# A transformer block on one core: head and tail of the instruction streams in another order, and some attention outputs in other PSUM banks

## The chip, the cores and the metric

The kernel runs on one core of a Trainium2 chip. The core has five engines, each of which works through its own list of instructions in order: TensorE (PE, matrix products), VectorE (DVE), ScalarE (ACT), GpSimd (POOL) and SyncE (SP), which issues the DMA transfers here. They meet through semaphores: an instruction counts one up when it is done, and another engine waits for a count. The metric is the device time of one execution in microseconds; the median of three runs counts.

## The reference

A pre-layernorm block on x of 1024 tokens by 256 features, all in float32:

```python
x = x + attention(layernorm(x))   # 16 heads of 128, rotary q and k, window of 128 keys, softmax, output projection wo
x = x + ffn(layernorm(x))         # 256 -> 1024, exact gelu, 1024 -> 256; weights rounded to -1, 0, 1
```

A query sees only the 128 keys up to its own position, so a tile of 128 queries needs the keys of its own tile and of the one before.

## The kernel before

Each float32 product is made of three products of halves: an operand is split into a `hi` part (a cast, on ScalarE) and a `lo` part (the rest, a subtraction on VectorE or GpSimd). So a tensor that TensorE is to use costs two more instructions on two engines: `qkhi`/`qklo` for the weights of q and k of a head, `vhi`/`vlo` for the value weights of a pair of heads, `xt_hi`/`xt_lo` for the transposed input, `rothi`/`rotlo` for rotated q or k, `ot_hi`/`ot_lo` for the attention output. All engines have their order written out by hand.

The work runs over 64 chunks and 64 steps. A chunk m projects q or k of a head for half of the tokens (`project(m)`, L385). VectorE multiplies it by sine (`times_sin`, L717, L719) and cosine (`times_cos`), SP swaps the halves of the sine product by two DMA transfers (`swap`, L287), the sum is `rotate` (on VectorE, L735, for the first two chunks, on GpSimd, L949, for the rest), then come `rothi` on ScalarE (L589) and `rotlo` (VectorE L740 for the first two, GpSimd L954 after). A step n handles 256 queries of one head: `scores(n)` on TensorE (L435), `merge(n)` on VectorE (L748, L751, L754: the windowed scores and their maximum), `exps(n)` on ScalarE (L594), `inverse_sum(n)` on VectorE (L759), `scale_probs(n)` on ScalarE (L601), `transpose_probs(n)` on TensorE (L446), `mask_pt(n)` on VectorE (L765), `weigh_v(n)` on TensorE (L460), then `ot_hi(n)` on ScalarE (L613) and `ot_lo(n)` on VectorE (L772). In step n TensorE does the scores of n, the transposition and weighing of n - 1, the projection of chunk n + 4 and a filler, if there is one: `project_v` (L400, the values of 256 tokens for a pair of heads; ScalarE's `copy_v` takes them out of the bank) or `project_out` (L417, the output projection; VectorE's `add_out`, L778, adds it to x). Steps 2 to 6 have no filler; from step 7 on nearly every step has one. `LP` is 56, the first step of the last pair of heads; `PAIRS` is 8.

PSUM has eight banks: PR0, PR1 (projections), SC0, SC1 (scores), PT (transposed probabilities), OT (attention outputs), and VO0, VO1 (values and output projections, by turns). `weigh_v(n)` waits until `ot_lo(n - 1)` has read OT.

After the last step come the second layernorm (`tile_stats` L690, `moments` L696, L698, `rsqrt` on GpSimd L931, `normalise` L703), the transposition of x (`transpose_x`, L358), the two layers of the feed-forward part (`ffn1` L488, `ffn2` L507) and its splitting (`ghi` L802, `glo` L807), twice, once for each half of the tokens. The first of these stand among the last steps already.

The head of GpSimd's list, the part before its loop over the steps, reads

```python
rsqrt(0, 0); pool.wait_ge(xn_ready, 4); qklo(0); rsqrt(0, 1); vlo(0)
pool.wait_ge(rot_done, 2); rotate(2); qklo(1); pool.wait_ge(rotlo_done, 2)
```

and ScalarE's: `qkhi(0)`, `xt_hi(0, 0)`, `vhi(0)`, `copy_v(0)`, `xt_hi(0, 1)`, `copy_v(1)`, `rothi(0)`, `qkhi(1)`, `rothi(1)`, `rothi(2)`.

Of the kernel before, what the change touches and what calls it, by code (L numbers as in the profile page):

```python
# [5 lines left out]
P = 128  # L6
# [10 lines left out]
def preln_block_kernel(nc, x, wq, wk, wv, wo, w1t, b1, w2t, b2, cos_t, sin_t, in_prev, mask_t, ident, out):  # L17
    T, D = x.shape
    HD = P
# [15 lines left out]
    with ExitStack() as ctx:  # L35
# [186 lines left out]
        def before_in_bank(kind, i):  # L222
            at = in_banks.index((kind, i))
            earlier = [f for f in in_banks[:at] if f[1] % 2 == i % 2]
            return earlier[-1] if earlier else None

        def half_of(c):

            return slice((c // 2) * HALF, (c // 2 + 1) * HALF)
# [18 lines left out]
        def _(sp):  # L248
# [49 lines left out]
            load_table(0, cos_sb)  # L298
            load_table(1, sin_sb)
            load_table(1, cos_sb)  # L300
            load_head(1)
            swap(0)
            sp.dma_start(in_prev_sb[:], in_prev).then_inc(mask_in, 16)
            sp.dma_start(mask_sb[:].rearrange("p b q -> p (b q)"), mask_t).then_inc(mask_in, 16)
            swap(1)
            swap(2)
            sp.wait_ge(qklo_done, 1)
            load_head(2)
            swap(3)
            sp.wait_ge(vlo_done, 1)  # L310
# [32 lines left out]
        def _(pe):  # L343
# [46 lines left out]
            def project_v(v):  # L390
                p, c = v // 4, v % 4
                if c == 0:
                    pe.wait_ge(vlo_done, p + 1)
                bank_free("v", v)
                for i in range(2):
                    t = 2 * c + i
                    n = 0
                    for kd in range(KD):
                        for xt, wt in ((xT_hi, v_lo), (xT_lo, v_hi), (xT_hi, v_hi)):
                            last = mm(VO[v % 2][:, i * 256:(i + 1) * 256], xt[:, kd, t * P:(t + 1) * P], wt[:, kd],  # L400
                                      start=(n == 0), stop=(n == 3 * KD - 1))
                            n += 1
                last.then_inc(v_done, 1)
# [45 lines left out]
            def weigh_v(n):  # L449
                head, j = step(n)  # L450
                a = head % 2
                pe.wait_ge(pt_masked, n + 1)
                pe.wait_ge(v_copied, 4 * (head // 2) + j + 1)
                if n > 0:
                    pe.wait_ge(otlo_done, n)
                for i in range(2):
                    t = 2 * j + i
                    b0 = 1 if t == 0 else 0
                    for b in range(b0, 2):
                        last = mm(OT[:, i * P:(i + 1) * P], v_sb[:, t - 1 + b, a * HD:(a + 1) * HD],  # L460
                                  probsT[:, i, b], start=(b == b0), stop=(b == 1))
                last.then_inc(pv_done, 1)
# [59 lines left out]
            project(2, KD)  # L522
            project(3)
            for n in range(STEPS):
                scores(n)
                if n == MEANS_AT:
                    means_of_abs()
                if n > 0:
                    transpose_probs(n - 1)
                if n + 4 < CHUNKS:  # L530
                    project(n + 4)
                fill(n)
                if n == STEPS - 1:
                    transpose_x(1, 0)
                if n > 0:
                    weigh_v(n - 1)
            ffn1(0)
# [20 lines left out]
        def _(act):  # L558
# [51 lines left out]
            def ot_hi(n):  # L610
                head, j = step(n)
                act.wait_ge(pv_done, n + 1)
                copy(oT_hi(head)[:, 2 * j * P:(2 * j + 2) * P], OT[:, 0:256]).then_inc(othi_done, 1)  # L613

# [18 lines left out]
            xt_hi(0, 0)  # L633
            vhi(0)
            copy_v(0)
            xt_hi(0, 1)
            copy_v(1)
            rothi(0)
            qkhi(1)
            rothi(1)  # L640
            rothi(2)
            for n in range(STEPS):
                p, s = n // 8, n % 8
                if n >= 2:
                    ot_hi(n - 2)
                exps(n)
                if n == STEPS - 1:
                    xt_hi(1, 0)
                    ot_hi(n - 1)
                    nc.scalar.preload_act_table(ACT.Gelu)  # L650
                if n > 0:
                    for kind, i in fills(n - 1):
                        if kind == "v":
                            copy_v(i)
                scale_probs(n)
                if n + 3 < CHUNKS:
                    rothi(n + 3)
# [24 lines left out]
        def _(dve):  # L682
# [85 lines left out]
            def ot_lo(n):  # L768
                head, j = step(n)
                dve.wait_ge(othi_done, n + 1)  # L770
                ts = slice(2 * j * P, (2 * j + 2) * P)
                tt(oT_lo(head)[:, ts], OT[:, 0:256], oT_hi(head)[:, ts].bitcast(F32), ALU.subtract).then_inc(otlo_done, 1)  # L772

# [56 lines left out]
            times_cos(0)  # L830
            normalise(0, 1)
            times_sin(1)
            times_cos(1)
            rotate(0)
            xt_lo(0, 1)
            rotlo(0)
            rotate(1)
            dve.wait_ge(sin_in[1], 32)
            times_sin(2)
            rotlo(1)  # L840
            dve.wait_ge(cos_in[1], 16)
            times_cos(2)
            dve.wait_ge(nothing_set, 1)
            dve.wait_ge(mask_in, 32)
            nc.vector.copy_predicated(no_prev[:], in_prev_sb[:], nothing[:]).then_inc(no_prev_set, 1)
            times_sin(3)
            times_cos(3)
            dve.wait_ge(no_prev_set, 1)
            for n in range(STEPS):
                if n == STEPS - 2:  # L850
                    add_out(4 * PAIRS - 3)
                    tile_stats(1, 2)
                    tile_stats(1, 3)
                if n == STEPS - 1:
                    ot_lo(n - 2)
                    normalise(1, 0)
                merge(n)
# [4 lines left out]
                if 1 < n < STEPS - 1:  # L862
                    ot_lo(n - 2)
                if n == STEPS - 2:
                    moments(1, 0)
                if n + 4 < CHUNKS:
                    times_sin(n + 4)
                if n >= LP + 4:
                    for kind, w in fills(n - 1):
                        if kind == "o" and w != 4 * PAIRS - 3 and w != 4 * PAIRS - 4:  # L870
                            add_out(w)
                inverse_sum(n)
                if n + 4 < CHUNKS:
                    times_cos(n + 4)
                if 0 < n < LP + 4:
                    for kind, w in fills(n - 1):
                        if kind == "o":
                            add_out(w)
                if n == STEPS - 3:
                    add_out(4 * PAIRS - 4)  # L880
                    tile_stats(1, 0)
                    tile_stats(1, 1)
                if n == MEANS_AT:
                    thresholds()
# [10 lines left out]
            glo(1)  # L895
            add_out(4 * PAIRS - 2)
            tile_stats(1, 4)
            tile_stats(1, 5)
            ghi(2)
            glo(2)  # L900
            add_out(4 * PAIRS - 1)
            tile_stats(1, 6)
            tile_stats(1, 7)
            moments(1, 1)
            glo(3)
            ghi(4)
# [18 lines left out]
        def _(pool):  # L925
# [41 lines left out]
            pool.wait_ge(xn_ready, 4)  # L967
            qklo(0)
            rsqrt(0, 1)
            vlo(0)  # L970
            pool.wait_ge(rot_done, 2)
            rotate(2)
            qklo(1)
            pool.wait_ge(rotlo_done, 2)
# [60 lines left out]
```

## Time and profile before

| | |
|---|---|
| median of three runs | 361.02 us (360.62 to 361.49) |
| the profiled execution | 360.54 us |
| its span, first to last instruction | 358.8 us |
| TensorE busy | 340.5 us, 95% |
| VectorE, ScalarE, GpSimd busy | 263.8, 208.1, 223.5 us (74%, 58%, 62%) |
| mean granted clock of TensorE | 0.990 |

Busy shares are means over the span; products on TensorE are pipelined, so a busy TensorE is not one at its peak. Times within the profile count from the first instruction of the span.

### The profile page before, as it was taken

The page shows a single profiled execution, that of the slowest core. Times are in us where ns is not written, and L with a number is a line of the kernel's source. Part 1 is how long each engine was busy: PE and PEld are TensorE (multiplying, and loading weights), DVE is VectorE, ACT ScalarE, POOL GpSimd, SP SyncE. Part 2 cuts the span into 40 slices and gives each one's busy share as a digit, 9 for nine tenths or more (in the row PEclk, how much of TensorE's full clock was granted, in tenths as well). Part 3 has the DMA queues.
Part 4 walks back from the last instruction along what each step waited for, and adds up shares of the span by engine and source line. Part 5 has one row for each costly group of instructions (what it writes and reads, how often), then busy time and mean ns, then how long its engine had stood idle before and what let it go on. Part 6 is the DMA issues. An engine that isn't in the chain of part 4 may idle for free.

```text
span 358.8 us, 6923 instructions
## 1 busy us (share of the span) xinstructions
PE 340.5 (95%) x2410; PEld 315.1 (88%) x2410; DVE 263.8 (74%) x607; ACT 208.1 (58%) x626; POOL 223.5 (62%) x182
## 2 busy tenths in 40 slices
PE   7849999999999999999999999999999999898996
PEld 6738778999999999999999999999999999877986
DVE  4874777668766886788788986787678766788681
ACT  2243676677777556655665566556665666365180
POOL 2326778667767678799879987585867656231300
PEclk9997999999999999999999999999999999999999
DMA  7734466543333333333333333333322231000001
GB/s 220 188 95 114 117 164 197 130 102 78 92 83 86 80 84 84 88 81 89 88 90 88 90 88 90 90 89 90 88 61 58 61 88 31 0 3 0 31 29 58
DMA packets 29025, 31.25 MB, mean 87 GB/s; under 512 B 3392, under 2 KB 20288, under 8 KB 28992
## 3 DMA queue, kind: packets, MB, share of 16 engines
q1 hardware_dynamic: 28992, 30.82, 33.7%
q8 instruction: 19, 0.31, 0.4%
q14 instruction: 14, 0.11, 0.1%
HBM read 12.98 MB, written 1.05 MB: 39 GB/s over the span
## 4 chain that ended last, share of the span: by engine, by line
PE 84%; DVE 9%; POOL 2%; issue 2%; DMA 1%; ACT 1%; DVEq 0%; SPq 0%; POOLq 0%
PE PR L385 22%; PE OT L460 15%; PE VO L400 13%; PE SC L435 12%; PE VO L417 11%; PE PT L446 3%; PE PR L488 2%; PE SC L488 2%; PE VO L507 1%; DVE probsT L765 1%; PE SC L507 1%; DVE stats L690 1%; DVE SC L751 1%; DVE gT_lo L807 1%; DVE gT_lo L772 1%
## 5 line engine op out<-in xcount | busy, mean ns | idle before, releaser
L954 POOL TENSOR_TENSOR gT_lo<-turn,gT_hi 128x512 fp32r<-128x512 f32 x62 | 81.7, 1318 | 42.9 <-ACT gT_hi L589 42.7
L949 POOL TENSOR_TENSOR turn<-turn,swapped 128x512 f32<-128x512 f32 x62 | 80.2, 1293 | 38.2 <-DMA swapped<-by_sin 37.9
L594 ACT ACTIVATE probs<-SC,negmax 128x128 f32<-128x128 f32 x128 | 45.8, 363 | 61.9 <-DVE negmax L754 61.9
L460 PE MATMUL OT<-probsT,v_sb 128*128 128x128 f32 x480 | 64.6, 276 | 3.1 <-DVE gT_lo L772 2.7
L601 ACT ACTIVATE probs<-probs,rinv 128x128 f32<-128x128 f32 x128 | 44.5, 395 | 38.2 <-DVE rinv L759 38.2
L460 PEld LDWEIGHTS OT<-probsT,v_sb 128*128 128x128 f32 x480 | 58.9, 191 | 6.0 <-DVE probsT L765 6.0
L385 PE MATMUL PR<-xT_hi,qk_lo 128*128 128x512 f32 x128 | 56.2, 439 | 5.1 <-POOL qk_lo L936 3.7
L751 DVE COPY_PREDICATED SC<-in_prev_sb,SC 128x256 f32<-128x256 int32 x48 | 20.6, 428 | 45.7 <-PE SC L435 45.5
L385 PE MATMUL PR<-xT_hi,qk_hi 128*128 128x512 f32 x128 | 51.0, 398 | 0.0
L385 PE MATMUL PR<-xT_lo,qk_hi 128*128 128x512 f32 x128 | 50.4, 394 | 0.0
L765 DVE TENSOR_TENSOR probsT<-PT,mask_sb 128x512 f32<-128x512 f32 x64 | 43.6, 681 | 1.2 <-PE PT L446 1.2
L589 ACT CAST gT_hi<-turn 128x512 fp32r<-128x512 f32 x64 | 38.9, 607 | 8.5 <-POOL turn L949 7.6
L435 PE MATMUL SC<-gT_hi,gT_lo 128*128 128x256 f32 (+1 forms) x128 | 41.1, 321 | 0.4 <-DVE gT_lo L740 0.4
L400 PE MATMUL VO<-v_lo,xT_hi 128*128 128x256 f32 x128 | 36.7, 287 | 1.0 <-POOL v_lo L940 1.0
L417 PE MATMUL VO<-o_lo,gT_hi 128*128 128x256 f32 x128 | 36.3, 284 | 1.0 <-DVE xres L778 1.0
L400 PE MATMUL VO<-v_hi,xT_hi 128*128 128x256 f32 x128 | 36.6, 286 | 0.0
L400 PE MATMUL VO<-v_hi,xT_lo 128*128 128x256 f32 x128 | 36.5, 285 | 0.0
L417 PE MATMUL VO<-o_hi,gT_hi 128*128 128x256 f32 x128 | 36.0, 282 | 0.0
L435 PE MATMUL SC<-gT_lo,gT_hi 128*128 128x256 f32 (+1 forms) x128 | 36.0, 281 | 0.0
L435 PE MATMUL SC<-gT_hi 128*128 128x256 f32 (+1 forms) x128 | 35.9, 281 | 0.0
L417 PE MATMUL VO<-o_hi,gT_lo 128*128 128x256 f32 x128 | 35.9, 281 | 0.0
L385 PEld LDWEIGHTS PR<-xT_hi,qk_lo 128*128 128x128 f32 x128 | 24.3, 190 | 8.5 <-POOL qk_lo L936 3.9
(114 smaller groups left out, 839.1 us busy)
## 6 DMA issues: line engine op xcount, KB each, us to landing
swapped<-by_sin SPq DMA_DIRECT2D x128, 128.0 KB, 2.3
qk_raw<-in_wq SPq DMA_DIRECT2D x16, 128.0 KB, 2.6
qk_raw<-in_wk SPq DMA_DIRECT2D x16, 128.0 KB, 2.4
v_raw<-in_wv SPq DMA_DIRECT2D x8, 256.0 KB, 3.1
o_raw<-in_wo SPq DMA_DIRECT2D x8, 256.0 KB, 2.9
xres<-in_x SPq DMA_DIRECT2D x4, 256.0 KB, 3.2
w_raw<-in_w1t SPq DMA_DIRECT2D x4, 256.0 KB, 3.0
w_raw<-in_w2t SPq DMA_DIRECT2D x4, 256.0 KB, 3.0
```

Of the source, the lines that this page charges most:

```text
L385: last = mm(PR[m % 2][:], wt[:, c % 2, kd], xt[:, kd, half_of(c)], start=(n == 0), stop=(n == 3 * KD - 1))
L400: last = mm(VO[v % 2][:, i * 256:(i + 1) * 256], xt[:, kd, t * P:(t + 1) * P], wt[:, kd], start=(n == 0), stop=(n == 3 * KD - 1))
L417: last = mm(VO[w % 2][:, i * 256:(i + 1) * 256], ot[:, t * P:(t + 1) * P], wt[:, a], start=(n == 0), stop=(n == 5))
L435: last = mm(SC[n % 2][:, o0:(i + 1) * 256], q[:, t * P:(t + 1) * P], k[:, k0 * P:(t + 1) * P], start=(p_ == 0), stop=(p_ == 2))
L460: last = mm(OT[:, i * P:(i + 1) * P], v_sb[:, t - 1 + b, a * HD:(a + 1) * HD], probsT[:, i, b], start=(b == b0), stop=(b == 1))
L589: copy(rot_hi(head, c % 2)[:, half_of(c)], turn[m % 4][:]).then_inc(rothi_done, 1)
L594: nc.scalar.activation(probs[n % 2][:, i], SC[n % 2][:, i * 256 + P:(i + 1) * 256], ACT.Exp, bias=negmax[:, n % 2, i:i + 1], accum_out=row ...
L601: last = nc.scalar.activation(probs[n % 2][:, i], probs[n % 2][:, i], ACT.Copy, scale=rinv[:, n % 2, i:i + 1])
L751: nc.vector.copy_predicated(sc[:, :, 1], in_prev_sb[:].unsqueeze(1).broadcast_to([P, 2, P]), sc[:, :, 0]).then_inc(merged, 1)
L765: tt(probsT[:], PT[:, 0:256].rearrange("p (i q) -> p i q", i=2).unsqueeze(2).broadcast_to([P, 2, 2, P]), mask_sb[:].unsqueeze(1).broadcast ...
L949: tt(turn[m % 4][:], turn[m % 4][:], swapped[m % 2][:], ALU.add).then_inc(rot_done, 1)
L954: tt(rot_lo(head, c % 2)[:, half_of(c)], turn[m % 4][:], rot_hi(head, c % 2)[:, half_of(c)].bitcast(F32), ALU.subtract).then_inc(rotlo_don ...
```

## The change

No instruction is added or removed, and no size changes. On SP the load of head 1 goes ahead of the second cosine table, the two masks ahead of the first swap, and the load of head 2 ahead of the third swap. On TensorE `project(3)` and the filler of step 0 go behind `scores(0)`, and in step 63 the transposition of x goes ahead of the filler. `weigh_v` of steps 2 to 5 writes the banks VO0 and VO1 instead of OT, and `ot_hi` and `ot_lo` read them there; its waits and those of `project_v(4)` and `project_v(5)` follow. On ScalarE, VectorE and GpSimd the instructions ahead of the loop and those of the last steps stand in another order.

```diff
+        def ot_bank(n):
+            return VO[n % 2] if 2 <= n <= 5 else OT
...
             load_table(1, sin_sb)
+            load_head(1)
             load_table(1, cos_sb)
-            load_head(1)
-            swap(0)
             sp.dma_start(in_prev_sb[:], in_prev).then_inc(mask_in, 16)
             sp.dma_start(mask_sb[:].rearrange("p b q -> p (b q)"), mask_t).then_inc(mask_in, 16)
+            swap(0)
             swap(1)
-            swap(2)
             sp.wait_ge(qklo_done, 1)
             load_head(2)
+            swap(2)
...
# project_v(v), TensorE
+                if v in (4, 5):
+                    pe.wait_ge(otlo_done, v + 1)
                 bank_free("v", v)
...
# weigh_v(n), TensorE
-                if n > 0:
-                    pe.wait_ge(otlo_done, n)
+                if n in (2, 3):
+                    bank_free("v", n + 2)
+                elif n > 0:
+                    pe.wait_ge(otlo_done, {4: 3, 5: 4, 6: 2}.get(n, n))
-                        last = mm(OT[:, i * P:(i + 1) * P], v_sb[:, t - 1 + b, a * HD:(a + 1) * HD],
+                        last = mm(ot_bank(n)[:, i * P:(i + 1) * P], v_sb[:, t - 1 + b, a * HD:(a + 1) * HD],
...
# TensorE
             project(2, KD)
-            project(3)
             for n in range(STEPS):
                 scores(n)
+                if n == 0:
+                    project(3)
+                    fill(0)
                 if n == MEANS_AT:
                     means_of_abs()
                 if n > 0:
                     transpose_probs(n - 1)
                 if n + 4 < CHUNKS:
                     project(n + 4)
-                fill(n)
                 if n == STEPS - 1:
                     transpose_x(1, 0)
                 if n > 0:
+                    fill(n)
                     weigh_v(n - 1)
...
# ScalarE (ot_hi reads ot_bank(n))
             vhi(0)
+            qkhi(1)
             copy_v(0)
             xt_hi(0, 1)
+            rothi(0)
+            rothi(1)
             copy_v(1)
-            rothi(0)
-            qkhi(1)
-            rothi(1)
-            rothi(2)
             for n in range(STEPS):
                 p, s = n // 8, n % 8
                 if n >= 2:
                     ot_hi(n - 2)
+                if n == STEPS - 1:
+                    xt_hi(1, 0)
                 exps(n)
                 if n == STEPS - 1:
-                    xt_hi(1, 0)
                     ot_hi(n - 1)
...
                 scale_probs(n)
+                if n == 0:
+                    rothi(2)
...
# VectorE (ot_lo reads ot_bank(n))
             times_cos(0)
-            normalise(0, 1)
             times_sin(1)
             times_cos(1)
+            normalise(0, 1)
             rotate(0)
+            rotate(1)
             xt_lo(0, 1)
             rotlo(0)
-            rotate(1)
-            dve.wait_ge(sin_in[1], 32)
-            times_sin(2)
             rotlo(1)
-            dve.wait_ge(cos_in[1], 16)
-            times_cos(2)
             dve.wait_ge(nothing_set, 1)
             dve.wait_ge(mask_in, 32)
             nc.vector.copy_predicated(no_prev[:], in_prev_sb[:], nothing[:]).then_inc(no_prev_set, 1)
-            times_sin(3)
-            times_cos(3)
+            dve.wait_ge(sin_in[1], 32)
+            times_sin(2)
+            dve.wait_ge(cos_in[1], 16)
+            times_cos(2)
             dve.wait_ge(no_prev_set, 1)
             for n in range(STEPS):
                 if n == STEPS - 2:
                     add_out(4 * PAIRS - 3)
                     tile_stats(1, 2)
                     tile_stats(1, 3)
+                    moments(1, 0)
                 if n == STEPS - 1:
                     ot_lo(n - 2)
-                    normalise(1, 0)
                 merge(n)
...
                 if 1 < n < STEPS - 1:
                     ot_lo(n - 2)
+                if n == 0:
+                    times_sin(3)
+                    times_cos(3)
                 if n == STEPS - 2:
-                    moments(1, 0)
+                    normalise(1, 0)
                 if n + 4 < CHUNKS:
                     times_sin(n + 4)
-                if n >= LP + 4:
-                    for kind, w in fills(n - 1):
-                        if kind == "o" and w != 4 * PAIRS - 3 and w != 4 * PAIRS - 4:
-                            add_out(w)
                 inverse_sum(n)
...
-                if 0 < n < LP + 4:
+                if n <= LP + 4:
                     for kind, w in fills(n - 1):
-                        if kind == "o":
+                        if kind == "o" and n > 0:
                             add_out(w)
+                if n == LP + 4:
+                    add_out(4 * PAIRS - 7)
                 if n == STEPS - 3:
                     add_out(4 * PAIRS - 4)
                     tile_stats(1, 0)
                     tile_stats(1, 1)
+                if n == STEPS - 2:
+                    add_out(4 * PAIRS - 6)
...
             add_out(4 * PAIRS - 2)
+            ghi(2)
+            glo(2)
+            glo(3)
             tile_stats(1, 4)
             tile_stats(1, 5)
-            ghi(2)
-            glo(2)
             add_out(4 * PAIRS - 1)
             tile_stats(1, 6)
             tile_stats(1, 7)
             moments(1, 1)
-            glo(3)
...
# GpSimd
             qklo(0)
+            vlo(0)
             rsqrt(0, 1)
-            vlo(0)
             pool.wait_ge(rot_done, 2)
+            qklo(1)
             rotate(2)
-            qklo(1)
             pool.wait_ge(rotlo_done, 2)
```

## Rows read from the trace of the kernel before

**Rows 1.** The page: TensorE's granted clock, 40 slices of 9 us, in tenths.
```profile
PEclk9997999999999999999999999999999999999999
```

**Rows 2.** Busy time by stretches: engine columns, then clock, DMA share, GB/s.
```profile
24.00:28.00 4.00, 0.60 (x2) 0.50 (x3) 1.51 (x5) 1.33 (x5) 3.13 (x3) 0.64 0.77 215
48.00:60.00 12.00, 11.22 (x77) 9.80 (x77) 9.64 (x22) 8.26 (x27) 10.71 (x9) 1.00 0.60 168
80.00:120.00 40.00, 40.00 (x294) 37.70 (x293) 30.15 (x73) 27.96 (x92) 27.34 (x23) 1.00 0.35 87
```

**Rows 3.** Waits of TensorE: total us, times, longest.
```profile
PE PR L385 <- POOL qk_lo L936: 3.7, 1, 3.7
PE OT L460 <- DVE gT_lo L772: 2.7, 7, 0.5
PE PR L385 <- DVE xT_lo L711: 1.4, 1, 1.4
...
PE VO L417 <- DVE xres L778: 1.0, 1, 1.0
PE VO L400 <- POOL v_lo L940: 1.0, 1, 1.0
```

**Rows 4.** The chain that ended last, head: start, length, what.
```profile
13.97 3.13 PE VO L400 x24
17.10 0.78 PE SC L358 x7
...
19.36 1.64 PE PR L385 x6
...
24.87 1.26 POOL turn L949
26.13 1.23 POOL qk_lo L936
...
27.40 2.93 PE PR L385 x6
30.33 2.20 PE VO L400 x12
...
33.47 1.39 PE PR L385 x6
34.86 1.43 PE VO L400 x12
...
36.96 0.73 PE SC L435 x6
```

**Rows 5.** Timeline of VectorE: start, length, what.
```profile
22.00 0.69 DVE L740 TENSOR_TENSOR gT_lo<-turn,gT_hi 128x512 fp32r<-128x512 f32 x1
```

**Rows 6.** Timeline of ScalarE.
```profile
31.17 0.69 ACT L601 ACTIVATE probs<-probs,rinv 128x128 f32<-128x128 f32 x2 [3.68 <-DVE rinv L759]
31.77 0.60 ACT L589 CAST gT_hi<-turn 128x512 fp32r<-128x512 f32 x1
```

**Rows 7.** The chain that ended last, one of steps 2 to 6.
```profile
38.51 0.68 DVE probsT L765
39.19 0.34 DVE gT_lo L772
...
39.67 1.13 PE OT L460 x8
```

**Rows 8.** The chain that ended last, tail.
```profile
305.25 0.61 DVE xres L778
...
311.27 1.14 PE OT L460 x8
...
313.27 1.29 DVE xnorm L703 x4
...
315.39 0.81 ACT probs L594 x4
...
316.71 0.70 DVE xT_lo L711
```

More of the change, by code:

```diff
@@ L612, in ot_hi @@
                 act.wait_ge(pv_done, n + 1)
-                copy(oT_hi(head)[:, 2 * j * P:(2 * j + 2) * P], OT[:, 0:256]).then_inc(othi_done, 1)
+                copy(oT_hi(head)[:, 2 * j * P:(2 * j + 2) * P], ot_bank(n)[:, 0:256]).then_inc(othi_done, 1)
             def abs_sums(i):
@@ L771, in ot_lo @@
                 ts = slice(2 * j * P, (2 * j + 2) * P)
-                tt(oT_lo(head)[:, ts], OT[:, 0:256], oT_hi(head)[:, ts].bitcast(F32), ALU.subtract).then_inc(otlo_done, 1)
+                tt(oT_lo(head)[:, ts], ot_bank(n)[:, 0:256], oT_hi(head)[:, ts].bitcast(F32), ALU.subtract).then_inc(otlo_done, 1)
             def add_out(w):
```

## The prediction

> **What bounds the kernel now.** I read the page first, then the busy time by stretches, the waits of TensorE, and the chain of work that ended last. From 80 to 120 us TensorE is busy 40.00 of 40.00 us [rows 2], and the stretches up to 280 us look the same: the middle can only move as a whole. TensorE's own work is not touched by the change, so all there is to win is idle TensorE time and low clock at the head (before about 60 us) and at the tail (after 300 us).
>
> At the head there are three losses. First, TensorE waits 3.7 us, once, for `qk_lo` of head 1 [rows 3]. The chain says why: the GpSimd product `rotate(2)` starts at 24.87, released by the DMA swap of chunk 2, and only behind it, at 26.13, runs the subtraction that makes `qk_lo`; `project(4)` starts at 27.40 [rows 4]. Second, the clock: its mean is 0.64 in 24 to 28 us [rows 2], and the page's row of clocks has its one dip, a 7, in the fourth slice, 27 to 36 us [rows 1], right behind that idle time. 0.5 is the level 1.2 GHz, 1.0 is 2.4 GHz. Third, 2.7 us in seven waits for `gT_lo`, VectorE's `ot_lo` [rows 3]: the weighing of the values has one bank, OT, and cannot write it until `ot_lo` of the step before has read it.
>
> **The head, worked out.** Times are the span's, before to after.
>
> *Projection of the values.* `vlo(0)` goes ahead of `rsqrt(0,1)` on GpSimd, so the 1.0 us wait for `v_lo` [rows 3] goes: 13.97 becomes 13.0 [rows 4]. The price is that the second half's rstd comes about one GpSimd operation (1.25 us [rows 4]) later; it is hidden, because VectorE now works through the rotation products of chunk 1 before `normalise(0, 1)`, and TensorE needs the result only after 3.13 us of value products. If that cover were too short, the loss is at most the 1.0 us just won. So `project(2)` starts at 19.36 - 1.0 = 18.4 and ends at 20.0 [rows 4].
>
> *scores(0).* It no longer stands behind `project(3)`, but it needs `rotlo(1)`. VectorE has one more half of `xT_lo` and two `rotlo` after the release of `project(2)` at 18.25: three operations of 0.69 us [rows 5], partly overlapped, give 20.2. Then `scores(0)` with the extra 0.25 us of a product after a wait (1.64 against 1.39 [rows 4]) ends at 21.15; with `project(3)` 1.39, values 1.43, `project(4)` 1.39 [rows 4] the next, `scores(1)`, starts at 25.4. `project(4)` does not wait, since `qklo(1)` now waits only for the second rotation, which stands ahead of `xt_lo(0, 1)` on VectorE and so is done before 18, and for its cast, which is moved up on ScalarE as its load is on the SP queue. Before, `scores(1)` came after 30.33 + 2.20 = 32.53. The lead is 7.1 us. Clock included: the two groups at 1.2 GHz cost 2.93 - 1.64 = 1.3 and 2.20 - 1.43 = 0.8, that is 2.1 us of the 7.1.
>
> *What is late next.* `rothi(2)` is moved behind `scale_probs(0)` on ScalarE. That one waits for the reciprocal, which stands on VectorE behind `times_sin(4)`, which needs `project(4)` (done at 25.4). So: `times_sin(4)` to 26.1, scaling (0.69 [rows 6], with some 0.15 of handing over) to 26.95, `rothi(2)` 0.60 [rows 6] to 27.5, and then in order on GpSimd and ScalarE `rotlo(2)`, `rotate(3)`, `rothi(3)`, `rotlo(3)`: three GpSimd operations of 1.25 and one cast of 0.60, with hand-overs 4.6 us, to 32.1. `scores(2)` needs `rotlo(3)`. TensorE has work meanwhile until about 30.8 (a wait of 1 us for the scaled probabilities, then 0.22 for two transpositions, an estimate from 0.78 for seven [rows 4], 1.39, 1.43 and a weighing of less than 1.13). So it waits about 1.3 us and starts `scores(2)` at 32.1 instead of 36.96, with 0.25 for starting after a wait: lead 4.6 us. Behind `rothi(3)` on ScalarE the exponentials of step 1 queue, and `weigh_v(1)` keeps its wait on OT; I count no more than the lead of `scores(2)` there.
>
> *Steps 3 to 6.* `weigh_v(2)` to `weigh_v(5)` write VO0 and VO1, and need only `mask_pt`. In a step the mask product begins at 38.51 and lasts 0.68, then `ot_lo` 0.34, then the weighing starts at 39.67 [rows 7]. Without `ot_lo` in front, the weighing may start 0.34 earlier; the wait of one step is 2.7/7 = 0.39, so 0.05 is left. Four steps: 1.36 us. Bounds: 0 if the rotation (GpSimd, two operations each step and a third in every second one, 2.5 to 3.75 us against a new step of 3.5) becomes the limit, 4 x 0.39 = 1.56 above. I take 1.36, since over two steps GpSimd needs 6.25 of 7. The new waits cost nothing: the banks are idle here (the next values come at step 7), the copy of values 2 and 3 is a step or two old, and `ot_lo(2)` to `ot_lo(5)` are each done a step before the bank's next user. Lead after step 7: 4.6 + 1.36 = 6.0 us.
>
> *SP's queue.* Head 1 ahead of the second cosine table, and both masks ahead of the first swap, let transfers go sooner that nobody waited for; the swaps wait for VectorE's products anyway. `load_head(2)` ahead of `swap(2)` is issued while SP waits for `times_sin(2)`. Nothing, bounded by one transfer's issue.
>
> **A rule against it.** The row: after 3.7 us without work the clock fell, while after the 1.4 us wait for `xT_lo` ahead of `project(2)` it was still full (the slices up to 27 us show a 9) [rows 1, 3]. The Trainium skill, "TensorE: Matmul & The Clock Gate", section "What's actually happening", says that throttled is the default and activity releases it. By that rule read strictly, the new head, which has three waits of about 1 us where it had one long one, could fall to 1.2 GHz as well; by the row it does not, and the sum stands. That is a rival below, priced from rows.
>
> **The tail.** Four moves, one chain. (a) `add_out(25)` goes a step earlier. Now it runs from 305.25 to 305.86 [rows 8] and TensorE waits 1.0 for it [rows 3]; afterwards the same product waits for `ot_lo(59)`, which ends at 305.25, so 0.6 is won. (b) `moments(1, 0)` goes ahead of `merge(62)`, which takes some of this back, about 0.1: `weigh_v(61)` comes at 310.75 instead of 311.27 [rows 8]. (c) `normalise(1, 0)` leaves its place ahead of `merge(63)` and follows `ot_lo(60)`: 310.6 + 1.29 [rows 8] = 311.9. The reciprocal of step 62 now queues behind it, so scaling ends at 312.8 and TensorE, which would be free at 312.5, waits 0.4 for it. (d) The transposition of x comes before the last filler: about 1.0 us (0.78 for seven [rows 4], and the release), to 314.0; two casts of 0.60 on ScalarE [rows 6] to 315.1; only then the exponentials of step 63, 0.81 [rows 8]. VectorE's reciprocal of step 63 stands ahead of `xt_lo(1, 0)`, so that starts at 316.0, against 316.71 [rows 8]. Lead 0.7. Bounds: 0, if the reciprocal or the table load falls later, and 1.29, if the whole `normalise` leaves the chain. Behind it `glo(3)` comes earlier, but VectorE has the same operations between the last `add_out` and the last `glo`, and TensorE needs that: the lead carries on, nothing is added.
>
> **Sum.** 6.0 + 0.7 = 6.7 us. The profiled execution took 360.54 us, of which its span is 358.8; 360.54 - 6.7 = 353.8. The median of the runs lies 0.48 above the profiled execution, so I forecast 354.3 us.
>
> **Rivals.**
> 1. *As worked out*: 354.3, own range 353.0 to 355.8. Chance 0.58.
> 2. *The clock falls again, or the rotation stays the limit to step 7*: the first costs up to 2.1 us, the second takes the 1.36 us. For it: three waits close together and GpSimd nearly full. Against: the waits are short. 355.8 to 357.8. Chance 0.20.
> 3. *Nothing is given back at `scores(2)`*, because `rotate(3)` or the scaling comes sooner than I have it: 7.1 instead of 4.6, that is 351.8. For it: all hand-overs above are rounded up. Against: `rothi(2)` is where it is. Chance 0.12.
> 4. *Slower: the low clock holds through the steps without fillers.* At 1.2 GHz a projection costs 1.3 us more; scores (0.73) and a weighing (about 0.9) would at most double, so a step costs up to 2.9 us more. Steps 1 to 6 would give 354.3 + 17 = 371. It decides from 6.7/2.9 = 2.3 such steps on. Against: in 48 to 60 us TensorE is idle a little in each step, 11.22 busy of 12, at a full clock [rows 2]. Chance 0.05. The rule named above would work in this way.
> 5. *The change does not do what it says*: `project(4)` waits all the same, because `qkhi(1)` or `rotate(1)` is late. Then the head wins the 1.0 and little else; within 1 us of 361. Chance 0.05.
>
> The range that leaves out no more than two in ten is 351.9 to 357.6. A measurement of this kernel can tell about 0.2% from no change, 0.7 us; faster by more than that: 0.90, within it: 0.04, slower: 0.06.
>
> **What the new profile would show.** Right: no wait of TensorE for `qk_lo`; granted clock 1.0 between 24 and 36 us; `scores(1)` at about 25, a wait of 1 to 2 us for `gT_lo` of the rotation at about 31; waits of the weighing for `gT_lo` down from seven to three or so, for `probsT` instead of it some 0.05; the first half of `xt_lo(1, 0)` 6.7 us earlier than 316.71. Wrong if: the clock row dips again; GpSimd runs without gaps from 32 to 54 us and TensorE waits for it at each second step; or the waits after 300 us are as long as now. The weakest term is the wait at `scores(2)`.

## The result and the profile after

The changed kernel takes 354.96 us (median of four runs, 354.6 to 356.06) against 360.82 us of the kernel before beside it: ratio 0.9844, 95% interval 0.9813 to 0.9875, 5.9 us. Forecast were 354.3 us and a range of 351.9 to 357.6. The profiled span went from 358.8 to 352.9 us. One run of all that are reported here, of the kernel with three banks, took 476.35 us at a mean granted clock of 0.659, and no comparison below uses it.

The page of the changed kernel: its span, busy time by engine, and the row of granted clocks in tenths, which answers to [rows 1].

```profile
span 352.9 us, 6925 instructions
...
PE 340.2 (96%) x2410; PEld 314.6 (89%) x2410; DVE 263.5 (75%) x607; ACT 208.1 (59%) x626; POOL 224.0 (63%) x182
...
PEclk9999999999999999999999999999999999999999
```

TensorE runs the same 2410 instructions, and the 7 in the fourth slice is gone. The busy time by stretches answers to [rows 2].

```profile
24.00:28.00 4.00, 3.13 (x19) 2.54 (x18) 2.52 (x6) 1.20 (x3) 1.63 (x2) 1.00 0.78 211
...
48.00:60.00 12.00, 11.56 (x81) 10.34 (x80) 8.98 (x22) 8.79 (x28) 10.25 (x9) 1.00 0.64 172
...
80.00:120.00 40.00, 40.00 (x296) 37.74 (x295) 30.16 (x73) 27.74 (x90) 26.91 (x22) 1.00 0.33 82
```

From 24 to 28 us TensorE worked 0.60 us before and works 3.13 now, at a full clock. The middle is full in both, so what is won at the head stays won. The waits of TensorE answer to [rows 3].

```profile
PE OT L468 <- DVE gT_lo L784: 1.6, 3, 0.6
PE PT L452 <- ACT probs L611: 1.5, 3, 0.9
PE VO L515 <- DVE gT_lo L819: 1.5, 2, 0.9
PE PR L389 <- DVE xT_lo L723: 1.4, 1, 1.4
PE SC L441 <- POOL gT_lo L967: 1.3, 1, 1.3
```

The wait for `qk_lo` has no row any more, and that for `v_lo` is down from 1.0 to 0.2. Of the seven waits for `ot_lo` three are left. New are a wait of 1.3 us of the scores for `rotlo` and three for the scaled probabilities (the longest 0.9). In the feed-forward part the second layer now waits twice for `glo`, 1.5 us together; before, the first layer waited 1.1 us for it and the second 0.5. How far the work of the changed kernel is ahead, by the timeline of TensorE (first product of each group) and, in the last row, of VectorE:

| | before | after | lead | forecast |
|---|---|---|---|---|
| `scores(1)` | 32.36 | 25.25 | 7.1 | 7.1 |
| `scores(2)` | 36.71 | 32.18 | 4.5 | 4.6 |
| `scores(3)` | 40.56 | 36.30 | 4.3 | 4.6 |
| `scores(7)` | 55.77 | 50.16 | 5.6 | 6.0 |
| `scores(8)` | 60.41 | 55.45 | 5.0 | 6.0 |
| `scores(60)` | 298.59 | 293.59 | 5.0 | 6.0 |
| `weigh_v(63)` | 320.86 | 315.16 | 5.7 | 6.7 |
| last sum of the output | 355.68 | 349.84 | 5.8 | 6.7 |

Up to `scores(7)` the lead grows again from 4.26 to 5.61, that is 1.35 us; from there to `scores(8)` 0.65 us of it are lost.

Next the chain that ended last, at the head of the changed kernel; its first rows answer to those of [rows 4] and [rows 6], the last three to [rows 7].

```profile
13.17 3.14 PE VO L406 x24
...
18.56 1.64 PE PR L389 x6
...
24.02 1.40 PE PR L389 x6
...
26.25 0.69 ACT probs L611 x2
26.94 0.52 ACT gT_hi L599
...
27.59 1.29 POOL gT_lo L967
28.88 1.25 POOL turn L962
30.13 0.69 issue
...
30.86 1.27 POOL gT_lo L967
...
33.92 0.62 ACT qk_hi L582
34.54 0.28 ACT gT_hi L623
...
34.84 0.44 DVE gT_lo L784
...
35.41 1.13 PE OT L468 x8
```

`project(4)` starts at 24.02 without a wait and takes 1.40 us, where it took 2.93. From there on the chain leaves TensorE: scaling, `rothi(2)`, `rotlo(2)`, `rotate(3)`, `rothi(3)`, `rotlo(3)` one behind the other, the very row that the prediction wrote down, up to 32.1. Behind it stands what the prediction left out: on ScalarE `ot_hi(0)` (34.54) comes only behind `rothi(4)` and `qkhi(2)` (33.92), and `weigh_v(1)` starts at 35.41.

The same chain in steps 5 to 7:

```profile
43.73 3.11 DMA swapped<-by_sin
...
46.91 1.30 POOL turn L962
...
48.75 0.61 ACT qk_hi L582
49.37 0.28 ACT gT_hi L623
...
50.01 0.68 DVE by_sin L729
50.69 0.09 DVE rinv L771
...
50.80 0.70 ACT probs L611 x2
...
51.55 0.44 PE PT L452 x2
```

A swap lands, `rotate` follows, its cast on ScalarE, behind that `qkhi(3)`, behind that `ot_hi(4)`. VectorE waits in its queue for it with `ot_lo(4)`, and behind `ot_lo(4)` stand the sine product and the reciprocal of the step. So the scaled probabilities, and with them TensorE, come late by way of an operation for which no bank waits any more.

This is where the 0.65 us are lost. TensorE's timeline has the first product of `scores(7)` and the transposition behind it, first in the kernel before:

```profile
55.77 0.36 PE L435 MATMUL SC<-gT_hi,gT_lo 128*128 128x256 f32 x1
...
56.56 0.38 PE L446 MATMUL PT<-ident_sb,probs 128*128 128x128 f32 x2
```

and in the changed one:

```profile
50.16 0.36 PE L441 MATMUL SC<-gT_hi,gT_lo 128*128 128x256 f32 x1
...
51.55 0.44 PE L452 MATMUL PT<-ident_sb,probs 128*128 128x128 f32 x2 [0.44 <-ACT probs L611]
```

From one to the other it is 0.79 us before and 1.39 after. The swap at the head of that chain took 3.11 us to land, where the page's median for swaps is 2.3. In the profile of "The old tail" below, whose instructions are the same up to there, it took 2.37: the transposition then comes 1.08 us behind `scores(7)`, and `scores(8)` starts at 55.11 instead of 55.45.

The tail, chain that ended last, answers to [rows 8].

```profile
305.69 1.29 DVE xnorm L715 x4
...
309.08 1.08 ACT xT_hi L575 x2
310.15 0.71 ACT probs L604 x4
...
311.06 0.60 DVE xT_lo L723
```

`xt_lo(1, 0)` starts at 311.06 instead of 316.71, a lead of 5.65 where `scores(60)` had 5.0.

### The profile page after: what moved, and what is told of

It reads as the page before. It is cut to its first block, busy times and chain, and to the rows that moved or that the text cites. A ratio compares the mean times of both kernels' runs of the same rounds, so it can differ in the third digit from the quotient of the medians.

```text
span 352.9 us, 6925 instructions
## 1 busy us (share of the span) xinstructions
PE 340.2 (96%) x2410; PEld 314.6 (89%) x2410; DVE 263.5 (75%) x607; ACT 208.1 (59%) x626; POOL 224.0 (63%) x182
## 4 chain that ended last, share of the span: by engine, by line
PE 83%; DVE 6%; DMA 2%; POOL 2%; ACT 2%; issue 2%; SPq 1%; DVEq 0%; POOLq 0%
PE PR L389 22%; PE OT L468 13%; PE VO L406 13%; PE SC L441 12%; PE VO L423 11%; PE PT L452 4%; PE PR L496 2%; PE SC L496 2%; DMA v_raw<-in_wv 2%; PE VO L515 1%; PE SC L515 1%; POOL turn L962 1%; DVE gT_lo L819 1%; DMA swapped<-by_sin 1%; DVE xnorm L715 1%
## 5 line engine op out<-in xcount | busy, mean ns | idle before, releaser
L468 PE MATMUL OT<-probsT,v_sb 128*128 128x128 f32 x450 | 60.2, 275 | 1.6 <-DVE gT_lo L784 1.6
L468 PEld LDWEIGHTS OT<-probsT,v_sb 128*128 128x128 f32 x450 | 55.3, 192 | 2.7 <-DVE probsT L777 2.7
L389 PEld LDWEIGHTS PR<-xT_hi,qk_hi 128*128 128x128 f32 x128 | 24.0, 187 | 5.6
```

The source lines that it names most:

```text
L389: last = mm(PR[m % 2][:], wt[:, c % 2, kd], xt[:, kd, half_of(c)], start=(n == 0), stop=(n == 3 * KD - 1))
L468: last = mm(ot_bank(n)[:, i * P:(i + 1) * P], v_sb[:, t - 1 + b, a * HD:(a + 1) * HD], probsT[:, i, b], start=(b == b0), stop=(b == 1))
```

## The experiments

The ratios are to the kernel before on the same chip, in brackets the 95% interval; leads and starts come from the profiled execution of each kernel. Profiled executions with the same instructions up to the tail differ at `scores(8)` by 0.1 to 0.4 us (one bank: 56.07 and 55.94; two: 55.45 and 55.11; three: 54.15 to 54.53), so differences of that size say little.

**One bank again.** In the changed kernel `ot_bank` gives OT for all steps, and the waits are those of before.

```diff
-            return VO[n % 2] if 2 <= n <= 5 else OT
+            return OT
...
-                if v in (4, 5):
-                    pe.wait_ge(otlo_done, v + 1)
...
-                if n in (2, 3):
-                    bank_free("v", n + 2)
-                elif n > 0:
-                    pe.wait_ge(otlo_done, {4: 3, 5: 4, 6: 2}.get(n, n))
+                if n > 0:
+                    pe.wait_ge(otlo_done, n)
```

> The changed kernel with all weighings in OT again and the waits of before; head and tail stay changed. Theory, that the banks are worth what the lead gained between weigh_v(1) (4.26 us) and scores(8) (4.97 us) in the new trace: 0.7 us longer than the changed kernel, waits of the weighing for gT_lo back at about 0.39 us in steps 3 to 6. The prediction's own term: 1.36 us longer. Rival, that the rotation alone sets these steps: no difference (below 0.2 us).

Measured: 356.92 us, 0.9888 [0.9865, 0.9911]. The waits of the weighing for `ot_lo` are seven again, 3.2 us. `scores(2)` starts at 32.11, as with two banks (32.18), `scores(7)` at 51.42 instead of 50.16, `scores(8)` at 56.07 instead of 55.45. So the banks are worth 1.3 us up to `scores(7)` and 0.6 at `scores(8)`, or 1.0 there against the profile of "The old tail". With one bank step 7 takes nothing back: the lead over the kernel before is 4.33 at `scores(3)` and 4.34 at `scores(8)`. The medians lie 2.0 us apart, more than that; the profile shows a part of the rest. Its busy time in single microseconds of the tail (TensorE's share is the second number after the stretch, the clock the third from the end):

```profile
327.00:328.00 1.00, 0.29 (x2) 0.29 (x3) 1.00 (x3) 0.00 (x0) 0.87 (x2) 1.00 0.00 0
328.00:329.00 1.00, 0.45 (x4) 0.24 (x3) 0.96 (x3) 0.00 (x0) 1.00 (x2) 1.00 0.00 0
...
330.00:331.00 1.00, 1.00 (x8) 1.00 (x7) 0.00 (x0) 0.00 (x0) 0.00 (x0) 0.63 0.06 16
331.00:332.00 1.00, 1.00 (x7) 1.00 (x6) 0.00 (x0) 0.11 (x1) 0.00 (x0) 0.50 0.00 0
```

The waits for `glo(5)` and `glo(7)` leave TensorE at 0.29 and 0.45, and then, with TensorE at full work again, the clock falls to 0.5 until about 334 us. From `weigh_v(63)` to the last sum this execution needs 1.6 us longer than the changed kernel's, with the same list of instructions there. Four of the six runs have a mean clock of 0.994 or 0.995 (356.9 to 358.3 us), two of 0.999 and 1.0 (355.9 and 356.2). Even these two lie 0.9 and 1.3 us above the changed kernel's median. So 0.6 to 1.0 us is the banks and some of the rest the fall in the tail; how much, the medians don't show.

**The banks alone.** The kernel before with `ot_bank` as changed, its uses and waits, and no other edit.

```diff
-                        last = mm(OT[:, i * P:(i + 1) * P], v_sb[:, t - 1 + b, a * HD:(a + 1) * HD],
+                        last = mm(ot_bank(n)[:, i * P:(i + 1) * P], v_sb[:, t - 1 + b, a * HD:(a + 1) * HD],
```

> The kernel before with the two banks for the weighings of steps 2 to 5 and nothing else. Theory, that the banks brought less than 1.36 us in the changed kernel because the rotation is late there, while it is 3.2 us ahead of scores(2) in the kernel before: 1.1 to 1.4 us shorter than before. Rival, that GpSimd's load in a step of 3.5 us is the limit in any order: about 0.7 us shorter. Rival, that the banks do nothing: 0.

Measured: 359.98 us, 0.9976 [0.9963, 0.9990]. `scores(2)` starts at 36.66 (before 36.71), `scores(8)` at 59.59 (60.41): 0.8 us. `scores(4)` and `scores(5)` gain 0.44 and another 0.40, as forecast or more; `scores(7)` is 1.16 ahead, `scores(8)` only 0.82. My theory, that the late rotation of the new head is to blame, is wrong: without the new head the banks bring no more. Here too step 7 takes some of it back, 0.34 us.

**Two casts later.** In the changed kernel the casts of the weights of heads 2 and 3 stand behind the exponentials of the next step on ScalarE.

```diff
                 exps(n)
+                if n == 2:
+                    qkhi(2)
+                if n == 6:
+                    qkhi(3)
...
-                if s == 1 and p < PAIRS - 1:
+                if s == 1 and 0 < p < PAIRS - 1:
                     qkhi(2 * p + 2)
...
-                if s == (4 if p == PAIRS - 2 else 5) and p < PAIRS - 1:
+                if s == (4 if p == PAIRS - 2 else 5) and 0 < p < PAIRS - 1:
                     qkhi(2 * p + 3)
```

> The changed kernel with the two casts qkhi(2) and qkhi(3) on ScalarE, about 0.5 us each in the queue, moved from the end of steps 1 and 5 to behind the exponentials of steps 2 and 6. Theory, that ot_hi queues on ScalarE behind the cast of the rotation and behind these, and that VectorE's ot_lo holds up the next products and so the probabilities: weigh_v(1) 0.5 us earlier in the profile, TensorE's longest wait for the probabilities 0.4 instead of 0.9 us, scores(8) 0.8 to 1.0 us earlier than 55.45. Rival, that the rotation itself (swap, rotate, rotlo) is the limit and these casts stand in its shadow: scores(8) within 0.2 us of 55.45.

Measured: `scores(2)` at 32.10, `weigh_v(1)` 0.3 us earlier (0.5 expected), `scores(3)` at 35.97 (36.30), `scores(8)` at 54.53 (55.45), 0.92 us earlier; span 352.0 instead of 352.9. The waits of TensorE in this kernel:

```profile
PE OT L468 <- DVE gT_lo L788: 1.4, 3, 0.6
...
PE SC L441 <- POOL gT_lo L971: 1.3, 1, 1.3
...
PE PT L452 <- ACT probs L611: 1.0, 2, 0.9
```

One wait for the probabilities is gone, 0.5 us in total; the longest, 0.9, is that of step 1, not of step 6 as I had taken it. From `scores(2)` to `scores(8)` it takes 22.43 us, the changed kernel 23.27 and the kernel before 23.70. With these casts out of the way the banks and the rest of these steps are worth 1.27 us against before, near the 1.36 of the prediction. Of the 0.92 us, 0.33 come at `weigh_v(1)` and 0.46 in step 7. So ScalarE's queue is a link in what took the difference. How large a part is its own isn't shown: against the profile of "The old tail", where the swap landed sooner, the gain at `scores(8)` is 0.58 us, and no run moves these casts with one bank. The median, 355.06 us, 0.9857 [0.9841, 0.9873], doesn't resolve 0.9 us from the changed kernel's; two of its four runs have a clock of 0.995.

**`qklo(1)` alone.** The kernel before with two moves:

```diff
# ScalarE
+            qkhi(1)
             rothi(0)
-            qkhi(1)
             rothi(1)
             rothi(2)
...
# GpSimd
+            qklo(1)
             rotate(2)
-            qklo(1)
```

> The kernel before with two instructions moved and nothing else: on GpSimd qklo(1) ahead of rotate(2), on ScalarE its cast qkhi(1) ahead of rothi(0). Theory, that this wait and the clock behind it are nearly the whole head: no wait for qk_lo, clock 1.0 up to 36 us, scores(1) at about 26.5 and, because the rotation becomes the limit, scores(2) at about 32; 4.3 us shorter than before, near 356.6. Rival, that only the wait of 3.7 us goes and the clock falls all the same: at most 3.7 us, with the dip still in the row of clocks. Rival, that the whole new head order is needed: 2 us or less.

Measured: 357.11 us, 0.9895 [0.9877, 0.9913], 3.9 us. No wait for `qk_lo`, no dip in the row of clocks, `scores(1)` at 27.37, `scores(2)` at 32.64: lead 4.1 us. By `scores(3)` it is 3.4 and stays so. The price that I had not seen: `scores(0)` waits 1.4 us for `rotlo(1)`, for two reasons. `qkhi(1)` at 19.34 now stands ahead of `rothi(0)` on ScalarE, which starts 0.5 us later; and `rotlo(1)` on VectorE takes 1.21 us, in the kernel before 0.69, as the timeline of this kernel has it:

```profile
22.51 1.21 DVE L740 TENSOR_TENSOR gT_lo<-turn,gT_hi 128x512 fp32r<-128x512 f32 x1
```

```profile
21.91 1.27 POOL L936 TENSOR_TENSOR qk_lo<-qk_raw,qk_hi 128x512 fp32r<-128x512 f32 x1 [8.00 <-DVE turn L735]
```

GpSimd's `qklo(1)` runs from 21.91 to 23.18 beside it; in the kernel before GpSimd is idle there, until 24.87. So these two moves are two thirds of the change.

**The wait kept, TensorE kept busy.** The kernel before, with products of constants in the wait.

```diff
             for n in range(STEPS):
...
+                if n == 0:
+                    keep_warm(OT, 9)
                 if n + 4 < CHUNKS:
                     project(n + 4)
```

> The kernel before with nine products of constants (about 0.37 us each, into the idle bank OT) on TensorE ahead of project(4), which fill its wait of 3.7 us; the wait itself stays. Theory, that the low clock behind the wait costs 2.1 us by the rows at both levels: clock 1.0 from 24 to 36 us and 2.1 us shorter than before. Rival, that scores(2) waits for something else then and the clock cost is hidden: less than 0.5 us.

Measured: 359.00 us, 0.9948 [0.9928, 0.9969], 2.0 us; all starts from `scores(1)` to `scores(60)` lie 2.1 us earlier. The row of clocks on this kernel's page, and, from its waits of TensorE, what is left of the wait:

```profile
PEclk9999999999999999999999999999999999999999
```

```profile
PE PR L385 <- POOL qk_lo L938: 1.7, 1, 1.7
```

`project(4)` starts when it did (27.30, before 27.40), and nothing but the clock behind it is better. The price of 2.1 us that the prediction read from two rows at either level is what it costs. The products fill only 2.0 us of the wait, less than expected, and yet the clock stays at 1.00 through the 1.7 us that are left. In the kernel before it fell inside the wait, which began at 23.69: its mean is 1.00 from 24 to 25 us and 0.56 from 25 to 26.

**`vlo(0)` alone.** The kernel before with `vlo(0)` ahead of `rsqrt(0, 1)`.

```diff
+            vlo(0)
             rsqrt(0, 1)
-            vlo(0)
```

> The kernel before with vlo(0) ahead of rsqrt(0,1) on GpSimd and nothing else. Theory: project_v(0) starts 1.0 us earlier, and since project(2), its sine product, the swap, rotate(2) and qk_lo hang on it one behind the other, all of it moves: 1.0 us shorter. Rival, that the later rstd delays the second half's transposition by as much: 0.

Measured: 359.76 us, 0.9966 [0.9955, 0.9977], 1.2 us. `scores(0)` is 0.76 earlier, all from `scores(1)` on 1.2. The wait for `v_lo` goes from 1.0 to 0.3, and `project(4)` starts 0.75 us earlier. The other 0.5 us lie in the low clock behind it, where the page of this kernel shows an 8 instead of the 7.

**`rothi(2)` earlier.** The changed kernel with one line moved.

```diff
+                if n == 0:
+                    rothi(2)
                 scale_probs(n)
-                if n == 0:
-                    rothi(2)
```

> The changed kernel with one line moved: the cast rothi(2) on ScalarE stands ahead of scale_probs(0) instead of behind it. Theory, that this place is what makes rotlo(3) and so scores(2) late: scores(2) about 1.2 us earlier, its wait of 1.3 us for gT_lo gone or nearly, and the kernel 0.9 to 1.3 us shorter than the changed one, about 353.9. Rival, that the wait only moves to weigh_v(1), which needs ot_hi(0) behind rothi(4), or to the later steps: within 0.3 us of the changed kernel.

Measured: 354.74 us, 0.9851 [0.9814, 0.9888]. `scores(2)` starts at 30.33, 1.85 us earlier, and its wait is gone; `scores(3)` is 1.1 earlier, `scores(8)` 0.75, the span 352.2. So the place of `rothi(2)` does cause the wait, and more than half of what its removal wins is taken by the next ones: `weigh_v(1)` now waits 1.4 us for `ot_lo(0)`. The profiled execution is 1.0 us shorter than the changed kernel's, the median only 0.2, as the rival had it; the intervals overlap, so the runs don't resolve what the move is worth.

**Three banks.** The same, with OT, VO0 and VO1 by turns from step 1 on.

```diff
-            return VO[n % 2] if 2 <= n <= 5 else OT
+            return {1: VO[0], 2: VO[1], 4: VO[0], 5: VO[1]}.get(n, OT)
...
-                if n in (2, 3):
-                    bank_free("v", n + 2)
+                if n in (1, 2):
+                    bank_free("v", n + 3)
                 elif n > 0:
-                    pe.wait_ge(otlo_done, {4: 3, 5: 4, 6: 2}.get(n, n))
+                    pe.wait_ge(otlo_done, {3: 1, 4: 2, 5: 3, 6: 4}.get(n, n))
```

> The changed kernel with rothi(2) ahead of scale_probs(0), and with three banks by turns for the weighings of steps 1 to 6 (OT, VO0, VO1, OT, VO0, VO1, OT), so that weigh_v(1) doesn't wait for ot_lo(0) either. Theory, that ScalarE's queue behind the casts of the rotation sets these steps, whichever bank is free: scores(3) about 1.4 us earlier than with rothi(2) alone, but scores(8) within 0.5 us of it, and 354 us. Rival, that the wait of weigh_v(1) for OT was the limit: scores(8) 1.4 us earlier, 353.2.

Measured: 353.27 us, 0.9787 [0.9768, 0.9806]; this beats both kernels. `scores(3)` at 33.91, 1.3 earlier than with `rothi(2)` alone; `scores(8)` at 54.16, 0.5 earlier: the theory's figures for the starts, but the time is the rival's (353.2). The starts don't explain the further 0.9 us. Its profiled execution, 355.13 us, has a mean clock of 0.994 and an 8 in the 38th slice of clocks: behind the same two waits for `glo(5)` and `glo(7)`, 0.87 and 0.58 us, the clock is 0.5 from 329 to 331 us, and this tail too is 1.6 us longer than the changed kernel's. The other five runs, 352.9 to 353.6, have 0.999 or 1.0.

**The old tail.** The changed kernel with the tail of before on TensorE, ScalarE and VectorE; its core:

```diff
+                if n > 0:
+                    fill(n)
                 if n == STEPS - 1:
                     transpose_x(1, 0)
                 if n > 0:
-                    fill(n)
                     weigh_v(n - 1)
...
+                exps(n)
                 if n == STEPS - 1:
                     xt_hi(1, 0)
-                exps(n)
-                if n == STEPS - 1:
                     ot_hi(n - 1)
...
-                    moments(1, 0)
                 if n == STEPS - 1:
                     ot_lo(n - 2)
+                    normalise(1, 0)
...
                 if n == STEPS - 2:
-                    normalise(1, 0)
+                    moments(1, 0)
```

> The changed kernel with the tail of before on TensorE, ScalarE and VectorE. Theory, that the tail brought the difference of the leads at 294 us (5.0) and at the end (5.84): 0.8 us longer than the changed kernel. The prediction's term: 0.7. Rival, that the lead of the tail is only the head's, shifted: no difference.

Measured: 355.92 us, 0.9863 [0.9840, 0.9886], median 1.0 longer than the changed kernel. From `scores(60)` to the last sum it takes 57.05 us, as before (57.09), against 56.25 with the new tail. So the tail is worth 0.8 us.

**The old order of `glo`.** The kernel of three banks with one part of the tail undone.

```diff
-            ghi(2)
-            glo(2)
-            glo(3)
             tile_stats(1, 4)
             tile_stats(1, 5)
+            ghi(2)
+            glo(2)
             add_out(4 * PAIRS - 1)
             tile_stats(1, 6)
             tile_stats(1, 7)
             moments(1, 1)
+            glo(3)
```

> The kernel with three banks and rothi(2) early, with only the last part of VectorE's new order undone: the statistics of tiles 4 and 5 ahead of ghi(2), and glo(3) behind moments(1, 1) again. The prediction's view, that glo(3) ahead only moves the wait to the last glo: the same time as with it in runs without a dip, 353.2. Rival, that TensorE's early work there is won: 0.6 us longer. By the theory of the clock the waits lie apart again (1.1 us, then 0.5 four us later) and no run dips.

Measured: 353.94 us, 0.9822 [0.9786, 0.9858]. From `weigh_v(63)` to the last sum it takes 34.82 us, as before (34.82), against 34.68 in the changed kernel: `glo(3)` ahead wins 0.1. The four runs with a clock of 0.998 or more have a median of 353.3 us, as the prediction's view had it. Two of six runs have a clock of 0.995 all the same, so this order doesn't keep the clock up, and that part of the theory is wrong.

**Products of constants in the tail.** Two kernels, the one with one bank and the one with three, each with these lines in the second layer:

```diff
                 for f in range(NF):
+                    if g == 0 and f in (5, 7):
+                        pe.wait_ge(otlo_done, STEPS)
+                        keep_warm(OT, 2 if f == 5 else 1)
```

> The changed kernel with one bank for all weighings, whose profile shows a clock of 0.5 from 330 to 334 us behind two waits of TensorE (0.88 and 0.59 us) in the first half of the second layer; added are three products of constants into the idle bank OT ahead of those two waits, two and one, which fill them. Theory, that the waits of the new tail, which lie closer together than those of before, let the clock fall in some executions: clock 0.998 or more in all runs (it was 0.994 or 0.995 in four of six), and the median 1 us shorter, about 355.9. Rival, that the dips have another cause: clocks as before, median within 0.4 us of 356.9.

> The kernel with three banks and rothi(2) early, with the same three added products. By the first theory its runs all lie at 352.9 to 353.6 and none at 355; median 353.2, the one with the dip gone. By the rival one run in six stays at 355.

Measured: 356.79 us, 0.9887 [0.9863, 0.9910], and 355.15 us, 0.9842 [0.9820, 0.9866]: the first as without the products, the second 1.9 longer. With one bank the clocks are 0.997 to 1.0 now, and still the runs spread from 355.3 to 357.7, so the clock in the tail isn't the whole spread. The median stays 1.8 us above the changed kernel's, more than the profiles show for the banks; what makes up the rest is open. With three banks one run has 0.995. Its profile shows another part: the last transfer of the output, for which all other profiles here show 1.4 us, took 2.8:

```profile
SPq L35 <- DMA out_y<-xnorm: 2.8, 1, 2.8
```

Its last sum starts at 349.02, and the span ends at 353.5. Whether the products cause that, these runs don't tell.

## Why the prediction was right, and where it was off

*The waits and the clock at the head.* Right in mechanism and size: lead at `scores(1)` 7.1, as forecast. The two moves of `qklo(1)` alone bring 3.9 us and `vlo(0)` alone 1.2; of the head's gain 2.1 is clock, shown by keeping TensorE busy through a part of the same wait. Two readings were off without harm to the sum: the clock fell not behind 3.7 us without work but inside them, and of the seven waits for `ot_lo` only five, 2.0 us, lie in the head; the other two, 0.37 and 0.36 us, stand at 301.55 and 311.27 us.

*What is late next.* Right: the row from `rothi(2)` to `rotlo(3)` ends at 32.1, the wait is 1.3 us, and the one-line move shows that the place of `rothi(2)` is the cause.

*`weigh_v(1)`.* "I count no more than the lead of `scores(2)` there" was a term set to zero: it costs 0.3 us, since `ot_hi(0)` queues behind `rothi(4)` and `qkhi(2)`.

*Steps 3 to 6.* The mis-sized term: 1.36 us forecast, 0.70 left at `scores(8)`; 0.6 to 1.0 by taking the banks away, 0.8 by adding them alone. Up to `scores(7)` the term came out, 1.35. What failed is that the prediction carried this lead through step 7 as it was: there the transposition waits for the scaled probabilities, and 0.65 us go. The bound below was argued from GpSimd's busy time in a step. The chain that bound runs from the swap by way of `rotate` and its cast into ScalarE's queue, with 8.26 of 12 us busy before [rows 2] not a suspect by its share: `ot_hi` stands behind a cast that waits for the rotation. The bank no longer waits for `ot_lo`, but VectorE's next products do, by order. Taking two casts out of that queue gives 0.9 back in the profile, 0.46 of it in step 7; a swap that landed 0.7 us sooner gave 0.3. No run tells how the loss divides between the links.

*The tail.* Forecast 0.7 up to `xt_lo(1, 0)`, 0.65 there and 0.7 at `weigh_v(63)`; another 0.1 comes behind, where I had forecast nothing.

*The rivals.* The clock didn't fall at the head, in spite of waits of 0.9, 1.3 and 0.6 us, as the row had it. It did fall in the new tail in the profiles with one bank and with three, behind two waits of 0.9 and 0.6 us, where I had not looked for it. Of rival 2 the other half came half true: the rotation, by way of its casts, took back 0.65 of the 1.36 us. The Trainium skill, "TensorE: Matmul & The Clock Gate", section "What's actually happening", says that throttled is the default and that activity releases the throttle; the strict reading that I put with rival 4 was true of the tail in these two profiles, and not of the head. It doesn't decide the sign there, as it costs 1.6 us.

The sum, from lead to lead: 7.11 at `scores(1)`, - 2.58 at `scores(2)`, - 0.27 at `weigh_v(1)`, + 0.70 up to `scores(8)`, + 0.04 up to `scores(60)`, + 0.70 up to `weigh_v(63)`, + 0.14 behind it make 5.84 us in the profile, 6.7 forecast.

## What to carry to other kernels

Before a wait on a buffer is taken away, look for what else stands behind the same instruction in its engine's queue: here the free banks brought their 1.3 us, and half of it was lost one step later, because `ot_lo`, no longer needed by TensorE, still stood ahead of VectorE's next products, behind a late swap and the casts on ScalarE. An idle gap of TensorE has two prices, the wait and the low clock behind it; filling it with useless products measures the second by itself. And what an earlier cast frees is partly taken back: `qkhi(1)` ahead of `rothi(0)` made that one 0.5 us later, and with `rothi(2)` earlier `weigh_v(1)` became the next to wait.

## What the runs showed of the hardware

What the low clock costs varies between executions of one kernel. The kernel before has runs with a mean clock of 0.990 and 0.995; of the 14 runs of it that four of the experiments (`qklo(1)` alone, the kept wait, `vlo(0)` alone, three banks) were compared with, those at 0.994 or 0.995 took 360.0 to 360.8 us, those at 0.990 or 0.991 360.4 to 361.6. With the wait filled, the four runs have 0.998 or 1.0. Two short waits close together, 0.9 and 0.6 us, with TensorE at 0.29 and 0.45 of two microseconds, were followed by 0.5 of the clock in the profile with one bank, and with three banks as well; in the changed kernel's, with the same two waits, the clock stayed full.

A subtraction of VectorE whose operands are all in SBUF took 1.21 us beside one of GpSimd and 0.69 us with GpSimd idle. In the kernel before, the first of the four instructions of `normalise(0, 1)`, whose operands are in SBUF too, took 1.11 us beside `vlo(0)` on GpSimd, and the next three 0.40 each. A product that reads PSUM, beside the same `qklo(1)`, took its usual 0.69. That the two engines are in each other's way at SBUF is what these pairs suggest; no run here separates it.
